# Layer 2's block stages: the bound of k plus u on VectorE in place of GpSimd, and new orders of both stages' work

## The chip, the cores and the metric

The kernel runs on one core of a Trainium2 chip: TensorE (PE), VectorE (DVE), ScalarE (ACT), GpSimd (POOL) and SyncE (SP), which issues most of the DMAs. The metric is the time of one execution on the device in microseconds; lower is better. Names as in the code: P = 128 partitions, TIME = 512 time steps, CH = 512 channels, BATCH = 4, UNITS = 16 units of a recurrence (4 groups of 128 channels by 4 batches), NB = 39 blocks of 128 token slots.

## What is computed

Four layers in a row change x of 4 x 512 x 512 float32. Each one runs a bidirectional decayed recurrence (WKV) over time, gates it with the sigmoid of x and puts the result through a feed-forward part that is added to x. Layer 2's feed-forward part is a mixture of 8 experts of which each token takes two. The recurrence reads the same k and v in every layer; v is k here.

```python
ek  = exp(minimum(k, 30)); ekv = ek * v
# nf, df: a = a*decay + ekv_t, b = b*decay + ek_t over time; nb, db: the same backwards
euk = exp(minimum(u + k, 30))
num = nf + nb - ekv + euk * v
den = df + db - ek + euk
out = sigmoid(r) * (num / maximum(den, 1e-8)) * (0.8 + 0.2 * tf)

# layer 2, feed-forward
scores = softmax(x @ W_gate.T); w, i = top_k(scores, 2)
eo = (silu(x @ gate_proj) * (x @ up_proj)) @ down_proj     # for each expert
y  = sum(eo[i] * w / sum(w)) + x
```

The backward scan is written so that it leaves out the step's own term, so no ekv and ek are subtracted.

## The kernel before

`experts` is layer 2's feed-forward part, from routing to the experts' outputs. It first routes the tokens and writes them to DRAM sorted by expert, in 39 blocks of 128 slots. Then come the two block stages that the change touches.

The gate/up stage, A, has eight turns (A_TURNS) of five blocks. A block is loaded from DRAM (`load_block`, into one of three buffers moe_zt), transposed on TensorE (`cols_of_z`), split into a high and a low part (`z_high` on ScalarE, `z_low` on VectorE), multiplied with the expert's gate and up weights in 12 matmuls (`gate_up`), gated (`silu` on ScalarE, `hidden` on VectorE) and written to DRAM (`store_hidden`, from one of two buffers moe_sg). A passage loads and splits the down weights, which lie in x's place meanwhile, since x is parked in DRAM; SyncE fetches them in eight pieces of 512 KB, one at the end of each of the turns 1 to 8 (`load_down`).

The down stage, B, has eight turns of five blocks too: `load_hidden` (four buffers moe_hb, 128 KB each), `cols_of_h` (two transposes), `h_high` and `h_low`, six matmuls (`down`), `out` on ScalarE (three buffers, those of moe_zt) and `store_out` (256 KB). At the end of the turns 1 to 4 SyncE issues `unpark`, which brings back a quarter of x, 1 MB.

Beside the blocks both stages carry layer 3's recurrence, one unit of 128 x 512 a turn: `w` eight units in A with one set of buffers, `v` eight units in B with two sets, which lie in columns of wh and wl, so that the trace calls its tiles moe_wh and moe_wl. A unit's steps, by engine: SyncE loads k (`load_k`, line 408) and exp_k and exp_k times v (`load_ek`, 414 and 415), 256 KB each; the bound `eu = min(k + u, 30)` (`bound`, 470); the exponential on ScalarE (`exps`, 349); GpSimd's product eu * k (`products`, 359), its sum into the forward numerator (`num_u`, 397) and with the backward one (`num_later`, 403); on VectorE the forward and backward scans (`scan_alone`, 384 and 389), the sum of both denominators (`both`, 476) and with eu (`den`, 482); ScalarE's `take_den`, `ln`, `recip_exp` (498, 506, 515); VectorE's `newton` (524, 526) and `quotient` (532); SyncE's `store` of the ratio (541), 256 KB.

The order on each engine is written out by hand. Each engine runs one loop over turns j, and `block_a(j, lag, q)` or `block_b(j, lag, q)` is block q of five of turn j - lag, or none; `unit_a` and `unit_b` are the same for units. So "third block" below is q = 2 of lag 1, and the next turn's first is q = 0 of lag 0. Every step waits for the semaphores of what it reads and of the buffer that it writes. All waits and issues of an engine are in order: on SyncE a DMA behind a waiting one waits too. The DMAs of SyncE share one queue (q1). `bound` waits for k and, of the unit that had the buffer before, for `den` and `newton`; `load_ek` waits for that unit's scans, `load_k` for its `num_u`, `load_block` for `cols_of_z` three blocks before, `load_hidden` for `cols_of_h` four before, `silu` for the hidden store two before, `h_high` and `h_low` for `down` two before.

## Time and profile before

| | us |
|---|---|
| timed runs | 1832.17, 1837.15, 1837.28 |
| their median | 1837.15 |
| the profiled execution | 1831.05 |
| its span, first to last instruction | 1829.2 |
| busy in the span: TensorE, VectorE, ScalarE, GpSimd | 1535.8, 1177.8, 983.6, 390.8 |
| mean granted clock of TensorE | 0.925 |

The span is one execution by the hardware profiler. Busy shares are means over four layers with different limits, so for a change in two stages the stages' own windows are read, and the waits in them.

### The profile page before, as it was taken

Reading aid. Unit: us, or ns where it says so; the run is one execution under the profiler, and the core shown is the slowest. Engines: PE = TensorE matmul, PEld = TensorE weight load, DVE = VectorE, ACT = ScalarE, POOL = GpSimd, SP = SyncE. Lnnn points to the kernel's source line nnn. Section 1 sums busy time; section 2 is a strip of 40 time slices with the busy share of each in tenths; the row PEclk is TensorE's granted clock in tenths of the full one; section 3 lists DMA queues with packets and bytes.
Section 4 is the critical chain, followed back from the end, with each engine's and each line's share of the span. In section 5 each row is a group of like instructions: output and inputs, shape, how many; then the busy total and the mean of one; then the engine's idle time right before and its main releaser. Section 6 shows DMA issues by size and latency. Waiting matters only on the chain. (4 is left out here: it accounts for less than half of the span.)

```text
span 1829.2 us, 21312 instructions
## 1 busy us (share of the span) xinstructions
PE 1535.8 (84%) x6839; PEld 1060.4 (58%) x6872; DVE 1177.8 (64%) x1888; ACT 983.6 (54%) x1313; POOL 390.8 (21%) x283
## 2 busy tenths in 40 slices
PE   5665778899977999996379957739999999999997
PEld 2222334444434666656357745538888888888886
DVE  7998688899987999986747777855422222222222
ACT  6764788899966999975246754524321221121210
POOL 0000111111200000004823334662032312322211
PEclk9998888899998999995579978979999999999999
DMA  7864633212103333327765648673010001101002
GB/s 282 278 197 166 241 104 104 81 59 69 53 12 128 120 104 109 113 75 267 281 198 188 201 158 277 240 253 115 1 35 35 35 1 35 35 0 35 1 12 81
DMA packets 117904, 218.54 MB, mean 119 GB/s; under 512 B 12708, under 2 KB 39588, under 8 KB 115364
## 3 DMA queue, kind: packets, MB, share of 16 engines
q1 hardware_dynamic: 112100, 199.34, 32.1%
q0 software_dynamic: 5120, 16.78, 2.6%
q8 instruction: 59, 0.97, 0.2%
q10 hardware_dynamic: 576, 1.05, 0.2%
q14 instruction: 49, 0.40, 0.1%
HBM read 149.10 MB, written 68.03 MB: 119 GB/s over the span
## 5 line engine op out<-in xcount | busy, mean ns | idle before, releaser
L2534 ACT ACTIVATE ffn_h<-ffn_pg,ffn_gate_chunk 128x512 f32<-128x512 f32 x64 | 44.0, 687 | 324.5 <-PE ffn_pg L2611 275.6
L2697 DVE SCALAR_TENSOR_TENSOR ffn_h<-ffn_pu,ffn_up_scale,ffn_h 128x512 f32<-128x512 f32 x64 | 48.1, 751 | 231.6 <-PE ffn_pu L2611 231.5
L2707 DVE SCALAR_TENSOR_TENSOR x<-ffn_po,ffn_out_scale,x 128x512 f32<-128x512 f32 x128 | 87.2, 744 | 149.3 <-PE ffn_po L2630 149.3
L2585 POOL TENSOR_TENSOR ffn_hl<-ffn_h,ffn_hh 128x512 fp32r<-128x512 f32 x64 | 82.5, 1289 | 413.2 <-ACT ffn_hh L2541 413.2
L960 POOL TENSOR_TENSOR l_rr<-l_rr,constants 128x1 f32<-128x1 f32 x32 | 28.8, 901 | 482.8 <-DVE l_rr L987 482.8
L2630 PE MATMUL ffn_po<-ffn_hh,ffn_wh 128*128 128x512 f32 x256 | 101.1, 395 | 3.5 <-DVE x L2707 2.9
L2611 PE MATMUL ffn_pg<-zhi,ffn_wh 128*128 128x512 f32 x256 | 101.6, 397 | 0.0
L2611 PE MATMUL ffn_pg<-zhi,ffn_wl 128*128 128x512 f32 x256 | 101.2, 395 | 0.0
L2611 PE MATMUL ffn_pu<-zhi,ffn_wh 128*128 128x512 f32 x256 | 101.1, 395 | 0.0
L2611 PE MATMUL ffn_pu<-zhi,ffn_wl 128*128 128x512 f32 x256 | 101.1, 395 | 0.0
L2611 PE MATMUL ffn_pu<-zlo,ffn_wh 128*128 128x512 f32 x256 | 101.1, 395 | 0.0
L2611 PE MATMUL ffn_pg<-zlo,ffn_wh 128*128 128x512 f32 x256 | 101.0, 395 | 0.0
L2630 PE MATMUL ffn_po<-ffn_hh,ffn_wl 128*128 128x512 f32 x256 | 100.6, 393 | 0.0
L2630 PE MATMUL ffn_po<-ffn_hl,ffn_wh 128*128 128x512 f32 x256 | 100.2, 392 | 0.0
L2195 POOL TENSOR_TENSOR x<-x,moe_zr 128x512 f32<-128x512 f32 x16 | 21.8, 1380 | 302.5 <-DVE moe_zr L2237 302.4
L2541 ACT ACTIVATE ffn_hh<-ffn_h 128x512 fp32r<-128x512 f32 x64 | 40.1, 627 | 83.5 <-DVE ffn_h L2697 83.5
L1965 PE MATMUL moe_bank<-moe_wh,moe_zhi 128*128 x156 | 65.1, 417 | 0.7 <-ACT moe_zhi L2093 0.7
L1965 PE MATMUL moe_bank<-moe_wh,moe_zlo 128*128 x156 | 62.5, 401 | 0.0
L1965 PE MATMUL moe_bank<-moe_wl,moe_zhi 128*128 x156 | 62.4, 400 | 0.0
L369 DVE TENSOR_TENSOR_SCAN wkv_fd<-decay,wkv_ek 128x512 f32<-128x512 f32 x48 | 58.4, 1216 | 2.9 <-DMA wkv_ekv<-exp_k_times_v 2.9
L814 PE MATMUL l_pa<-l_row_b,l_diag 128*128 128x512 f32 x128 | 58.2, 597 | 2.4 <-ACT l_diag L890 2.4
L369 DVE TENSOR_TENSOR_SCAN wkv_fn<-decay,wkv_ekv 128x512 f32<-128x512 f32 x48 | 58.4, 1216 | 0.0
(381 smaller groups left out, 4412.3 us busy)
## 6 DMA issues: line engine op xcount, KB each, us to landing
wkv_k<-in_fside SPq DMA_DIRECT2D x56, 256.0 KB, 3.7
ratio<-wkv_fn SPq DMA_DIRECT2D x56, 256.0 KB, 2.1
wkv_ek<-exp_k SPq DMA_DIRECT2D x40, 256.0 KB, 3.3
wkv_ekv<-exp_k_times_v SPq DMA_DIRECT2D x40, 256.0 KB, 3.9
moe_zt<-tokens_by_slot SPq DMA_DIRECT2D x39, 256.0 KB, 3.2
expert_out<-moe_zt SPq DMA_DIRECT2D x39, 256.0 KB, 2.3
moe_wl<-in_moe_up SPq DMA_DIRECT2D x16, 512.0 KB, 8.2
ffn_raw<-in_gated SPq DMA_DIRECT2D x8, 1024.0 KB
```

Of the source, the lines that this page charges most:

```text
L369: eng.tensor_tensor_scan(forward[:, :], decay.to_broadcast([P, TIME]), values[:, :], 0.0, op0=ALU.mult, op1=ALU.add)
L814: eng.matmul(p_a[:, m * 512:(m + 1) * 512], diag[p][:, :], rows["b1"][:, m * 512:(m + 1) * 512], start=True, stop=False)
L960: eng.tensor_tensor(out[p][:, :], out[p][:, :], c["minus_half"][:, :], ALU.pow).then_inc(*E(name).inc)
L1965: last = eng.matmul(p_gu[j % DEEP][:, :], z[j % 2][:, k * P:(k + 1) * P], part[:, k, ds(at, WCOL)], start=n == 0, stop=n == 3 * CT - 1)
L2195: eng.tensor_tensor(x_unit(n), x_unit(n), zr[n % ZRS][:, :], ALU.add).then_inc(*E("x_plus_z").inc)
L2534: eng.activation(hf[t][:, :], p_g[t][:, :], ACT.Silu, scale=scale).then_inc(*E(f"silu{t}").inc)
L2541: eng.activation(hh[t][slot % 2][:, :], hf[t][:, :], ACT.Copy).then_inc(*E(f"hh{t}").inc)
L2585: eng.tensor_tensor(hl[t][slot % 2][:, :], hf[t][:, :], hh[t][slot % 2][:, :].bitcast(F32), ALU.subtract).then_inc(*E(f"hl{t}").inc)
L2611: last = eng.matmul(ps[:, :], chunk_w(part, slot, which, k, t), z[:, k, tok], start=(n == 0), stop=(n == 3 * CT - 1))
L2630: last = eng.matmul(p_o[:, o, :], chunk_w(w, slot, "down", k, o), h[k][slot % 2][:, :], start=(n == 0), stop=(n == 3 * HT - 1))
L2697: eng.scalar_tensor_tensor(hf[t][:, :], p_u[t][:, :], scale, hf[t][:, :], ALU.mult, ALU.mult).then_inc(*E(f"h{t}").inc)
L2707: last = eng.scalar_tensor_tensor(x[:, o, :], p_o[:, o, :], out_s[:, o:o + 1], x[:, o, :], ALU.mult, ALU.add)
```

## The change

On VectorE `bound` is added in both stages and on GpSimd it is removed. In A it stands behind `quotient`, in B it is done one turn earlier than before (lag 0), between `both` and `den`. GpSimd runs `products`, `num_u` and `num_later` of a unit in that order in both stages. In B `exps` moves from near the front of ScalarE's turn to near its end, the last backward scan of a unit to the start of VectorE's next turn, and the ratio's store from the middle of SyncE's turn of lag 3 to the end of that of lag 2, ahead of `unpark`. The loads of k and exp_k, the stores of hidden and output blocks, and a few steps of TensorE and ScalarE change places as the diff shows. No computation changes.

```diff
--- before.py
+++ after.py
@@ -1845,24 +1845,24 @@
                     load_block(n)
                 for n in block_a(j, 1, 3):
                     load_block(n)
+                for n in block_a(j, 1, 4):
+                    load_block(n)
+                for u in unit_a(j, 1):
+                    w.load_k(eng, u, u % w.slots)
                 for u in unit_a(j, 1):
                     w.load_ek(eng, u, u % w.slots)
-                for n in block_a(j, 1, 4):
-                    load_block(n)
+                for n in block_a(j, 2, 4):
+                    store_hidden(n)
+                for n in block_a(j, 1, 0):
+                    store_hidden(n)
                 for n in block_a(j, 0, 0):
                     load_block(n)
-                for n in block_a(j, 2, 4):
-                    store_hidden(n)
-                for u in unit_a(j, 1):
-                    w.load_k(eng, u, u % w.slots)
-                for u in unit_a(j, 2):
-                    w.store(eng, u, u % w.slots)
-                for n in block_a(j, 1, 0):
-                    store_hidden(n)
                 for n in block_a(j, 0, 1):
                     load_block(n)
                 for n in block_a(j, 1, 1):
                     store_hidden(n)
+                for u in unit_a(j, 2):
+                    w.store(eng, u, u % w.slots)
                 for n in block_a(j, 1, 2):
                     store_hidden(n)
                 for n in block_a(j, 1, 3):
@@ -1870,33 +1870,33 @@
                 if 1 <= j <= DOWN_PIECES:
                     load_down(j - 1)
             eng.wait_ge(*E("gate_up").at(NB - 1))
-            for j in range(B_TURNS + 3):
+            for j in range(B_TURNS + 2):
                 for n in block_b(j, 1, 2):
                     load_hidden(n)
                 for n in block_b(j, 1, 3):
                     load_hidden(n)
+                for u in unit_b(j, 0):
+                    v.load_k(eng, u, u % v.slots)
                 for n in block_b(j, 1, 4):
-                    load_hidden(n)
-                for u in unit_b(j, 3):
-                    v.store(eng, u, u % v.slots)
-                for n in block_b(j, 0, 0):
-                    load_hidden(n)
-                for u in unit_b(j, 0):
-                    v.load_ek(eng, u, u % v.slots)
-                for n in block_b(j, 0, 1):
                     load_hidden(n)
                 for n in block_b(j, 2, 4):
                     store_out(n)
-                for u in unit_b(j, 0):
-                    v.load_k(eng, u, u % v.slots)
+                for n in block_b(j, 0, 0):
+                    load_hidden(n)
                 for n in block_b(j, 1, 0):
                     store_out(n)
                 for n in block_b(j, 1, 1):
                     store_out(n)
+                for n in block_b(j, 0, 1):
+                    load_hidden(n)
+                for u in unit_b(j, 0):
+                    v.load_ek(eng, u, u % v.slots)
                 for n in block_b(j, 1, 2):
                     store_out(n)
                 for n in block_b(j, 1, 3):
                     store_out(n)
+                for u in unit_b(j, 2):
+                    v.store(eng, u, u % v.slots)
                 if 1 <= j <= BATCH:
                     unpark(j - 1)
             v.stored(eng)
@@ -2024,10 +2024,10 @@
                     cols_of_z(n)
                 for n in block_a(j, 1, 1):
                     gate_up(n)
+                for n in block_a(j, 1, 2):
+                    gate_up(n)
                 for n in block_a(j, 1, 4):
                     cols_of_z(n)
-                for n in block_a(j, 1, 2):
-                    gate_up(n)
                 for n in block_a(j, 1, 3):
                     gate_up(n)
                 for n in block_a(j, 0, 0):
@@ -2049,10 +2049,10 @@
                     cols_of_h(n)
                 for n in block_b(j, 1, 2):
                     down(n)
+                for n in block_b(j, 0, 0):
+                    cols_of_h(n)
                 for n in block_b(j, 1, 3):
                     down(n)
-                for n in block_b(j, 0, 0):
-                    cols_of_h(n)
                 for n in block_b(j, 1, 4):
                     down(n)
 
@@ -2128,10 +2128,10 @@
                 if j == A_TURNS + 1:
                     for m in range(FIRST_DOWN):
                         down_high(m)
+                for n in block_a(j, 1, 1):
+                    z_high(n)
                 for u in unit_a(j, 2):
                     w.take_den(eng, u, u % w.slots)
-                for n in block_a(j, 1, 1):
-                    z_high(n)
                 for u in unit_a(j, 2):
                     w.ln(eng, u, u % w.slots)
                 for n in block_a(j, 1, 2):
@@ -2163,28 +2163,28 @@
                     h_high(n)
                 for u in unit_b(j, 2):
                     v.take_den(eng, u, u % v.slots)
-                for u in unit_b(j, 1):
-                    v.exps(eng, u, u % v.slots)
-                for n in block_b(j, 1, 2):
-                    h_high(n)
                 for u in unit_b(j, 2):
                     v.ln(eng, u, u % v.slots)
                 for n in block_b(j, 1, 0):
                     out(n)
+                for n in block_b(j, 1, 2):
+                    h_high(n)
                 for n in block_b(j, 1, 3):
                     h_high(n)
+                for n in block_b(j, 1, 1):
+                    out(n)
                 for u in unit_b(j, 2):
                     v.recip_exp(eng, u, u % v.slots)
-                for n in block_b(j, 1, 1):
+                for n in block_b(j, 1, 2):
                     out(n)
                 for n in block_b(j, 1, 4):
                     h_high(n)
-                for n in block_b(j, 1, 2):
-                    out(n)
+                for u in unit_b(j, 1):
+                    v.exps(eng, u, u % v.slots)
+                for n in block_b(j, 0, 0):
+                    h_high(n)
                 for n in block_b(j, 1, 3):
                     out(n)
-                for n in block_b(j, 0, 0):
-                    h_high(n)
                 for n in block_b(j, 1, 4):
                     out(n)
 
@@ -2212,21 +2212,17 @@
             first_set_over(eng)
             for j in range(A_TURNS + 1):
                 for u in unit_a(j, 1):
-                    w.bound(eng, u, u % w.slots)
-                for u in unit_a(j, 1):
                     w.products(eng, u, u % w.slots)
                 for u in unit_a(j, 1):
                     w.num_u(eng, u, u % w.slots)
                 for u in unit_a(j, 1):
                     w.num_later(eng, u, u % w.slots)
-            for j in range(B_TURNS + 2):
-                for u in unit_b(j, 1):
-                    v.bound(eng, u, u % v.slots)
-                for u in unit_b(j, 2):
+            for j in range(B_TURNS + 0):
+                for u in unit_b(j, 0):
+                    v.products(eng, u, u % v.slots)
+                for u in unit_b(j, 0):
                     v.num_u(eng, u, u % v.slots)
-                for u in unit_b(j, 1):
-                    v.products(eng, u, u % v.slots)
-                for u in unit_b(j, 2):
+                for u in unit_b(j, 0):
                     v.num_later(eng, u, u % v.slots)
 
         @block.vector
@@ -2379,40 +2375,44 @@
                     z_low(n)
                 for u in unit_a(j, 2):
                     w.newton(eng, u, u % w.slots)
+                for n in block_a(j, 1, 0):
+                    hidden(n)
                 for u in unit_a(j, 2):
                     w.quotient(eng, u, u % w.slots)
-                for n in block_a(j, 1, 0):
+                for u in unit_a(j, 1):
+                    w.bound(eng, u, u % w.slots)
+                for n in block_a(j, 1, 1):
                     hidden(n)
+                for n in block_a(j, 1, 3):
+                    z_low(n)
                 for u in unit_a(j, 1):
                     w.scan_alone(eng, u, u % w.slots, "scan_d", False)
-                for n in block_a(j, 1, 3):
-                    z_low(n)
-                for n in block_a(j, 1, 1):
-                    hidden(n)
                 for u in unit_a(j, 1):
                     w.scan_alone(eng, u, u % w.slots, "scan_d", True)
-                for u in unit_a(j, 1):
-                    w.both(eng, u, u % w.slots)
                 for n in block_a(j, 1, 4):
                     z_low(n)
                 for n in block_a(j, 1, 2):
                     hidden(n)
+                for u in unit_a(j, 1):
+                    w.both(eng, u, u % w.slots)
                 for n in block_a(j, 1, 3):
                     hidden(n)
-                for u in unit_a(j, 1):
-                    w.scan_alone(eng, u, u % w.slots, "scan_n", False)
                 for n in block_a(j, 0, 0):
                     z_low(n)
                 for u in unit_a(j, 1):
                     w.den(eng, u, u % w.slots)
                 for u in unit_a(j, 1):
-                    w.scan_alone(eng, u, u % w.slots, "scan_n", True)
+                    w.scan_alone(eng, u, u % w.slots, "scan_n", False)
                 for n in block_a(j, 1, 4):
                     hidden(n)
+                for u in unit_a(j, 1):
+                    w.scan_alone(eng, u, u % w.slots, "scan_n", True)
             for m in range(FIRST_DOWN, DOWN_PIECES):
                 down_low(m)
             v.set_ends(eng)
             for j in range(B_TURNS + 2):
+                for u in unit_b(j, 2):
+                    v.scan_alone(eng, u, u % v.slots, "scan_n", True)
                 for n in block_b(j, 1, 1):
                     h_low(n)
                 for u in unit_b(j, 1):
@@ -2424,21 +2424,21 @@
                 for n in block_b(j, 1, 3):
                     h_low(n)
                 for u in unit_b(j, 1):
-                    v.both(eng, u, u % v.slots)
-                for u in unit_b(j, 1):
-                    v.den(eng, u, u % v.slots)
-                for n in block_b(j, 1, 4):
-                    h_low(n)
-                for u in unit_b(j, 1):
                     v.scan_alone(eng, u, u % v.slots, "scan_n", False)
                 for u in unit_b(j, 2):
                     v.newton(eng, u, u % v.slots)
+                for n in block_b(j, 1, 4):
+                    h_low(n)
+                for u in unit_b(j, 2):
+                    v.quotient(eng, u, u % v.slots)
+                for u in unit_b(j, 1):
+                    v.both(eng, u, u % v.slots)
+                for u in unit_b(j, 0):
+                    v.bound(eng, u, u % v.slots)
+                for u in unit_b(j, 1):
+                    v.den(eng, u, u % v.slots)
                 for n in block_b(j, 0, 0):
                     h_low(n)
-                for u in unit_b(j, 1):
-                    v.scan_alone(eng, u, u % v.slots, "scan_n", True)
-                for u in unit_b(j, 2):
-                    v.quotient(eng, u, u % v.slots)
 
 
 def gated_ffn(core, c, d, ratio):
```

## Rows read from the trace of the kernel before

**Rows 1.** Chain of waits, 900 to 1210 us: start us, us, what.

```profile
1200.78 0.34 SPq L1543
```

**Rows 2.** Windows: stretch, length, busy (count) PE, PEld, DVE, ACT, POOL; PEclk, DMA, GB/s.

```profile
926.00:1068.00 142.00, 132.76 (x624) 105.53 (x624) 102.42 (x145) 93.03 (x138) 46.83 (x30) 0.97 0.60 187
...
1087.00:1198.50 111.50, 79.85 (x308) 56.64 (x308) 88.21 (x115) 52.52 (x108) 60.27 (x32) 0.87 0.69 236
```

**Rows 3.** The same view by turn in stage A.

```profile
950.00:968.70 18.70, 17.27 (x87) 13.76 (x85) 13.57 (x19) 13.06 (x20) 6.30 (x5) 1.00 0.64 201
...
1042.00:1060.00 18.00, 17.86 (x88) 14.45 (x87) 14.81 (x22) 13.26 (x20) 6.11 (x4) 1.00 0.68 215
```

**Rows 4.** Waits in stage A: waiter, releaser, us in total, times, longest.

```profile
PE moe_bank L1951 <- DMA moe_zt<-tokens_by_slot: 30.4, 10, 23.7
```

**Rows 5.** Timeline, TensorE in A: start, us, engine, line, operation [idle before <- releaser].

```profile
992.53 0.66 PE L1951 MATMUL moe_bank<-ident,moe_zt 128*128 128x128 f32 x4 [1.85 <-DMA moe_zt<-tokens_by_slot]
```

**Rows 6.** Timeline, SyncE's issues in the next turn of A.

```profile
1004.08 0.33 SPq L414 DMA_DIRECT2D wkv_ek<-exp_k  x1
...
1005.63 1.45 SPq L1808 DMA_DIRECT2D moe_zt<-tokens_by_slot  x2
...
1007.12 0.43 SPq L1812 DMA_DIRECT2D expert_hidden<-moe_sg  x1
```

**Rows 7.** Windows view by turn in stage B.

```profile
1098.90:1113.40 14.50, 10.35 (x39) 7.73 (x38) 8.86 (x14) 6.31 (x14) 4.28 (x3) 0.76 0.77 254
...
1142.00:1158.00 16.00, 12.03 (x43) 8.77 (x42) 10.61 (x16) 6.72 (x14) 7.62 (x5) 0.79 0.78 266
...
1170.00:1182.00 12.00, 9.83 (x41) 6.33 (x41) 11.66 (x15) 6.73 (x14) 8.40 (x5) 1.00 0.71 242
```

**Rows 8.** Timeline, TensorE in B, the third of four waits.

```profile
1132.28 0.69 PE L1980 MATMUL moe_bank<-ident,moe_hb 128*128 128x128 f32 x2 [2.85 <-DMA moe_hb<-expert_hidden]
```

**Rows 9.** Timeline, SyncE in the same turn of B.

```profile
1126.11 0.53 SPq L1794 DMA_DIRECT2D x<-x_park  x1
...
1126.75 1.76 SPq L1818 DMA_DIRECT2D moe_hb<-expert_hidden  x3
...
1129.50 0.32 SPq L541 DMA_DIRECT2D ratio<-moe_wl  x1
```

**Rows 10.** DMA landing of line 1794 (x returns), then of line 1822 (output blocks).

```profile
DMA to landing us min/median/max: 5.7/6.0/6.6
...
DMA to landing us min/median/max: 2.0/2.3/4.2
```

**Rows 11.** Line views: count, duration ns min/median/max, first and last start.

```profile
L341 DVE TENSOR_SCALAR wkv_eu<-wkv_k,u x48: 473/478/486, 10.5 to 791.2; 128x512 f32<-128x512 f32 x48
...
L470 POOL TENSOR_SCALAR moe_wh<-moe_wh,u x8: 2127/2980/2982, 1086.7 to 1180.8; 128x512 f32<-128x512 f32 x8
...
L476 DVE TENSOR_TENSOR moe_wl<-moe_wl x8: 681/684/1405, 1093.5 to 1186.8; 128x512 f32<-128x512 f32 x8
...
L482 DVE TENSOR_TENSOR moe_wl<-moe_wl,moe_wh x8: 691/692/1653, 1094.2 to 1188.3; 128x512 f32<-128x512 f32 x8
...
L532 DVE SCALAR_TENSOR_TENSOR moe_wl<-moe_wl,neg_gain x8: 720/1034/1035, 1113.8 to 1197.5; 128x512 f32<-128x512 f32 x8
```

**Rows 12.** ScalarE's waits in B.

```profile
ACT moe_wh L349 <- POOL moe_wh L470: 14.5, 7, 2.6
```

**Rows 13.** Timeline in a waiting turn of B, ScalarE and TensorE.

```profile
1123.78 0.39 ACT L2105 ACTIVATE moe_hhi<-moe_bank 128x256 fp32r<-128x256 f32 x1 [0.28 <-PE moe_bank L1996]
...
1124.06 0.59 ACT L2111 ACTIVATE moe_zt<-moe_bank 128x512 f32<-128x512 f32 x1
...
1124.92 0.38 PE L1980 MATMUL moe_bank<-ident,moe_hb 128*128 128x128 f32 x2
```

**Rows 14.** Timeline, VectorE at the end of B.

```profile
1186.53 0.39 DVE L2338 TENSOR_TENSOR moe_hlo<-moe_bank,moe_hhi 128x256 fp32r<-128x256 f32 x1
...
1197.52 0.75 DVE L532 SCALAR_TENSOR_TENSOR moe_wl<-moe_wl,neg_gain 128x512 f32<-128x512 f32 x1
```

## Prediction

> **What bounds the kernel now.** I read the page's chain first: it is followed back from the end and holds no line of layer 2. The block of layer 2 ends for all engines together; SyncE then issues the next layer's first load at 1200.78 us [rows 1], and everything behind it follows from there. So a microsecond won before that is a microsecond won at the end. Then the windows view by stages: the gate/up stage (A) runs from 926 to 1068 us, a passage follows in which the down weights are split, and the down stage (B) from 1087 to 1198.5 us [rows 2]. The diff touches A and B.
>
> **Stage A.** TensorE is the busy engine, 132.8 of 142 us [rows 2]. One block is 12 matmuls and 4 transposes, 16 instructions. Four windows from 950 to 1024 us, about a turn of five blocks each, hold 87, 82, 82 and 83 of them: 20.9 blocks in 74 us, 3.54 us each; the two after them, to 1060 us, hold 88 each: 11 blocks in 36 us, 3.27 us each (the rows show the first and the last of the six) [rows 3]. The difference is waiting. TensorE waits 30.4 us for token blocks, 23.7 of it for the stage's first, so 6.7 us inside it [rows 4]. The longest is 1.85 us at a turn's fifth block [rows 5]. The SyncE timeline tells why one is late: in the next turn the load of the fifth block stands behind the two loads of exp_k, which go out at 1004.08, when the last scan is through; so it is issued at 1005.63 with 512 KB ahead of it, and the late hidden block is stored at 1007.12 only [rows 6].
>
> **Stage B.** Two regimes. In the four turns from 1098.9 to 1158 us a turn takes 13.6 to 16 us and VectorE is busy for 8.9 to 10.6 of it; in the two from 1158 to 1182 VectorE is busy 11.7 of 12.0 us (the rows show the first and the last of the four, and the second of the two) [rows 7]. The first kind waits for a DMA: TensorE stands 3.58, 3.62, 2.85 and 3.29 us at the turn's third block (the third is shown) [rows 8]. Its load is issued at 1126.75, straight behind the 1 MB that brings x back (1126.11), and TensorE goes on at 1132.28 [rows 8, 9], 5.5 us after the issue where 256 KB can land in 2.0 [rows 10]. The four waits match the four transfers of x, which land in 5.7 to 6.6 us [rows 10]. With them gone the stage is VectorE's.
>
> **The change part by part.**
>
> *Bound on VectorE.* Elsewhere VectorE does the same 128x512 instruction in 0.478 us; GpSimd takes 2.98 for it in B [rows 11]. In A VectorE is busy 13.6 of 18.7 us [rows 3], so the 0.48 hide: zero. In B they hide in the four waiting turns and count in the three after them, and once ahead of the first low part, for which the first down product waits: 4 x 0.48 = **+1.9 us**. The upper bound: it could wait for a running GpSimd instruction as others do. The sum on line 482 takes 0.69 us alone and up to 1.65, so 0.48 + 0.96 = 1.44 us each [rows 11].
> What goes away: ScalarE waited 14.5 us for the bound in seven turns of B [rows 12]. In the waiting turns that lies inside TensorE's wait for the DMA, in the late ones VectorE had work all the time: zero.
> What VectorE pays to GpSimd: in a late turn line 476 takes 0.72 us more than alone, line 482 0.96, the quotient (line 532) 0.31 [rows 11], 2.0 in all. After the change GpSimd's products and numerator sum follow the exponential, which now stands late in ScalarE's turn, just where VectorE does quotient, both, bound and den. So the 2.0 stay. At best the two sums' 1.68 go, 5.0 us in three turns.
> The Trainium skill's page "SBUF — State Buffer", section "SBUF: two separate sides", says that VectorE and GpSimd take a shared port pair exclusively, so that the one that starts second blocks until the other is through. The 1.4 us of line 476, twice its 0.68 alone, agree with that. By that rule the moved bound could be blocked in its turn; with 1.44 us each the sum below would be 3.8 us larger.
>
> *Order in A.* The fifth block's load goes ahead of the recurrence's loads, the loads of k ahead of exp_k's, the store of the late hidden block ahead of two loads, the fifth block's transposes one product later on TensorE. The last scan goes behind the last hidden product, 0.4 us, and exp_k's loads wait that much longer, with nobody at them for 5 us. The ratio's write-back now passes in front of two hidden stores; the ratio is ready by then. If the 20.9 slow blocks run at 3.35 us, (3.54 - 3.35) x 20.9 = 4.0 us come back; at 3.27, 5.6; at least nothing, since the third block's load still follows the last hidden store and a weight load. I take **-4.0**.
>
> *Passage.* The same instructions behind the same last weight load: zero.
>
> *Order in B, the four turns in which x returns.* The chain is: the third block's transposes, the products, `out` of the turn's fourth block, its store, x's return, the load, its landing. Three things come into it. (a) ScalarE now does h_high of the next turn's first block ahead of that `out`, 0.28 us from its start to the next one's, and TensorE its transposes ahead of the fourth product, 0.38: 0.66 us [rows 13]. (b) SyncE issues the ratio's write-back between store and return, 0.32 us and a gap of 0.1 [rows 9]; before, it stood behind the three loads. (c) Its 256 KB drain ahead of the load. From 2.3 us for 256 KB and 6.0 for 1 MB [rows 10] it is 3.7 x 256/768 = 1.23 us; at the 254 and 266 GB/s of the rows' waiting turns [rows 7], it is 1.0, and less if the transfers overlap. I take 0.85; bounds 0 and 1.23. The first return has only (a), as no ratio is done by then, the other three have all: 0.66 + 3 x (0.66 + 0.42 + 0.85) = **+6.4**.
>
> *Tail.* From the last low part (1186.53) VectorE works 11.74 us until 1198.27 [rows 14]. Now come low part 0.34, scan 1.13, Newton 1.37, quotient 0.75 to 1.03, both 1.40 and den 1.65 if GpSimd meets them, then ScalarE's three steps, 2.2 with their gaps, Newton 1.37 and quotient 0.75: 10.6 to 11.2. I take **-0.6**.
>
> Sum: 1.9 - 4.0 + 6.4 - 0.6 = **+3.7 us**.
>
> **Against which time.** The profiled execution took 1831.05 us, 1.85 more than its span of 1829.2; the timed runs took 1832.17, 1837.15 and 1837.28. The profile lies 6.1 under their median. I set the sum against the middle of all four, 1834.7: **1838.4 us**. A measurement of this kernel can tell about 0.3%, 5.5 us, from no change.
>
> **Rivals.**
> *The write-back also delays the late turns (slower).* Place: the third block's load in the turns without x's return. It now has 0.66 + 0.42 + 0.85 = 1.9 us in front of it. From the point at which that makes it land later than VectorE's turn of 12.0 us needs it, TensorE stops there, at up to 1.9 us in three turns, 5.7; I take 4.5: 1842.9. For it: the DMA engines are 0.71 busy there [rows 7], and the load of k, which waits for GpSimd's numerator sum, is new ahead of the fourth block's. Against: TensorE has no such wait there now.
> *GpSimd lets VectorE be and the write-back costs nothing (faster).* The two sums run alone, -5.0; of B's chain only 4 x 0.66 = 2.6 stay; A returns 5.6; bound and tail as above: -5.6 + 2.6 - 5.0 + 1.9 - 0.6 = -6.7, 1828.0. For it: GpSimd's work in B falls by 2.98 us a turn. Against: its two sums follow the exponential closely.
> *It does nothing:* A's waits move to another block and B's keep their length, 1834.7. For it: the waits in A at a turn's third block hang on the last hidden store, which isn't issued earlier.
>
> **How the numbers follow.** Forecast 0.34, nothing 0.08, slower rival 0.30, faster rival 0.28; so within 0.3% 0.42, slower 0.30, faster 0.28. The forecast's own range is 1833.7 to 1840.2 (-1 to +5.5). As cases of both signs hold most of the chance, the whole range goes from just under the faster rival, 1827, to A at zero with B's full sum and most of the slower rival: 1834.7 + 7.7 + 4.5 = 1847.
>
> **What would show it.** A: in SyncE's timeline the fifth block's load right behind the fourth's; no wait of 1.85 us; the stage 138 us instead of 142. B: still four waits of TensorE for moe_hb, nearer 5 than 3.3 us, in turns of 15 to 16; line 470 on VectorE at 0.48; late turns of 12.5 us full of VectorE. Wrong if the four waits shrink (then the queue was not the chain), if lines 476 and 482 stay at 0.69 late in B (the faster rival), or if waits for moe_hb appear after 1160 us (the slower one).

## The result and the profile after

The changed kernel takes **1846.95 us** (median of six runs, 1844.12 to 1849.94), the kernel before 1836.85 (six runs, 1832.17 to 1841.37). The ratio is 1.0062, interval 1.0043 to 1.0081: **10.1 us slower**, where I had forecast 1838.4 with a range of 1827 to 1847 and 0.30 for slower. The forecast was 3.7 us on a base of 1834.7, which itself lay 2.2 us under the median of six.

The two traces lie further apart than the medians. The profiled execution of after took 1849.94 us with a span of 1848.1, 3.0 over its median; that of before lies 5.8 under the median of its now six runs. 10.1 + 3.0 + 5.8 = 18.9 us, which is the difference of the spans. The stages account for it so (A from the start of the first transposes to that of the last gate/up product, B from the start of the first down product to that of the last, the tail from there to SyncE's first issue for the next layer; all are read from starts given to 0.1 us):

| us | A and passage | B | tail | all the rest |
|---|---|---|---|---|
| before | 161.4 | 100.8 | 12.4 | 1554.6 |
| after | 159.7 | 117.9 | 12.1 | 1558.4 |

The rest holds nothing that the change touches, and moves between 1554.6 and 1567.1 us in the sixteen traces of this study. So experiments below are compared by their stages first, with the timed runs beside them. Two traces of the same code, `a_new_b_old` and `a_new_again`, have B and tail at 114.3 and 114.9 us.

Windows view of after: gate/up stage, passage, down stage, then four turns of the down stage, two in which x returns and the two late ones (columns as in rows 2):

```profile
928.00:1068.70 140.70, 132.90 (x624) 105.36 (x624) 106.80 (x153) 94.66 (x138) 34.47 (x22) 0.97 0.61 190
1068.70:1087.50 18.80, 1.38 (x4) 0.58 (x4) 14.46 (x21) 11.71 (x14) 3.35 (x2) 0.60 0.42 136
1087.50:1215.50 128.00, 86.53 (x308) 60.75 (x308) 101.25 (x118) 53.90 (x108) 34.56 (x24) 0.81 0.63 204
...
1101.90:1119.60 17.70, 10.72 (x41) 7.29 (x41) 12.70 (x17) 6.95 (x14) 4.21 (x4) 0.90 0.73 230
1119.60:1138.40 18.80, 12.00 (x40) 8.58 (x40) 13.09 (x17) 6.95 (x14) 4.50 (x4) 0.69 0.70 225
...
1172.80:1185.90 13.10, 10.31 (x42) 7.16 (x40) 12.56 (x16) 6.85 (x14) 4.12 (x4) 0.89 0.69 222
1185.90:1199.40 13.50, 10.53 (x41) 7.34 (x41) 12.61 (x16) 6.85 (x14) 4.11 (x4) 0.88 0.68 221
```

The turns with x's return took 13.6 to 16 us before, by the prediction's reading of [rows 7], and 16.8 to 18.8 now; the late ones grew from 12.0 to 13.1 and 13.5. The DMA share of the stage fell from 0.69 to 0.63 [rows 2]: the same bytes, over a longer time.

TensorE still waits four times for a hidden block, as in [rows 8]; timeline of after, the second of the four:

```profile
1124.65 0.69 PE L1980 MATMUL moe_bank<-ident,moe_hb 128*128 128x128 f32 x2 [4.25 <-DMA moe_hb<-expert_hidden]
```

and its load in SyncE's timeline (to set against [rows 9]):

```profile
1112.02 0.39 SPq L414 DMA_DIRECT2D moe_wh<-exp_k  x1
1112.46 0.42 SPq L415 DMA_DIRECT2D moe_wh<-exp_k_times_v  x1
1112.94 1.79 SPq L1822 DMA_DIRECT2D expert_out<-moe_zt  x2
1115.22 0.32 SPq L541 DMA_DIRECT2D ratio<-moe_wl  x1
1115.58 0.54 SPq L1794 DMA_DIRECT2D x<-x_park  x1
1116.21 1.62 SPq L1818 DMA_DIRECT2D moe_hb<-expert_hidden  x2
```

In this turn 9.1 us lie between the issue of x's return (1115.58) and TensorE's going on (1124.65), where the turn of [rows 8, 9] had 1132.28 - 1126.11 = 6.2. What stands ahead of the return was issued in the last 3.6 us: 512 KB of exp_k and its product, two output blocks, 256 KB of the ratio. x itself lands later than the 5.7 to 6.6 us of [rows 10], by the view of line 1794 of after:

```profile
DMA to landing us min/median/max: 7.6/8.2/8.6
```

These two points, the issue of line 1794 and TensorE's start behind the wait, cut the four turns into parts. I read them off the same two timelines for every return:

| us | first product to first return | return to TensorE, four times | TensorE to the next return, three times |
|---|---|---|---|
| before | 9.2 | 6.2, 7.0, 6.2, 6.6 | 8.5, 7.7, 7.6 |
| after | 10.4 | 8.6, 9.1, 8.7, 8.1 | 8.9, 9.7, 8.9 |
| difference | +1.2 | +8.5 | +3.7 |

Together +13.4 us (1087.61 to 1146.45 before, 1087.77 to 1159.98 after). From there to the last product come 3.8 more.

The four waits themselves hardly grew: 4.14, 4.25, 2.92 and 2.33 us make 13.6, where it was 13.3 before. The load lands later, but TensorE also gets to it later. In each of these turns it now stops for a low part on the way, 1.66 to 2.15 us, where in before it had no such stop above 0.7. VectorE and TensorE in the turn shown above:

```profile
1117.79 0.41 DVE L2334 TENSOR_TENSOR moe_hlo<-moe_bank,moe_hhi 128x256 fp32r<-128x256 f32 x1
...
1118.40 0.49 PE L1996 MATMUL moe_bank<-moe_wh,moe_hhi 128*128 x1 [1.66 <-ACT moe_hhi L2105]
```

This stop costs nothing here, as it lies inside the time from the return to the landing of the load. It also means that the length of these waits doesn't tell how late the load is.

### The profile page after: what moved, and what is told of

It is laid out like the page before. It is cut to its first block and busy times, and to the rows that moved or that the text cites. A ratio compares the mean times of both kernels' runs of the same rounds, so it can differ in the third digit from the quotient of the medians.

```text
span 1848.1 us, 21309 instructions
## 1 busy us (share of the span) xinstructions
PE 1547.2 (84%) x6839; PEld 1065.9 (58%) x6872; DVE 1195.7 (65%) x1904; ACT 986.9 (53%) x1313; POOL 354.2 (19%) x267
## 5 line engine op out<-in xcount | busy, mean ns | idle before, releaser
L1996 PE MATMUL moe_bank<-moe_wh,moe_hhi 128*128 x78 | 42.1, 539 | 20.0 <-issue 14.6
```

The source lines that it names most:

```text
L1996: last = eng.matmul(p_eo[j % DEEP][:, :], h[j % 2][:, k * P:(k + 1) * P], part[:, k, ds(at, CH)], start=n == 0, stop=n == 3 * HT - 1)
```

## The experiments

All ratios are against the kernel before, timed between them on the same chip.

**The stages apart.** Stage A of after, stage B of before, on all five engines (diffs are against after, where nothing else is said):

```diff
 # stage A: as in the change; stage B, SyncE (the other engines alike):
-            for j in range(B_TURNS + 2):
+            for j in range(B_TURNS + 3):
...
-                for u in unit_b(j, 2):
-                    v.store(eng, u, u % v.slots)
```

> Stage A of the changed kernel, stage B of the kernel before. Both theories put the loss in stage B: 1 to 3 us faster than before (stage A is 1.8 us shorter in the trace of the change, from its first block to the first down product). If stage A carries part of the loss, it comes out slower than before.

It took 1831.65 us, ratio 0.9955 (0.9938 to 0.9971), by its medians 5.5 us faster where 1 to 3 were expected. I ran the same code again beside later kernels:

> New stage A, old stage B, once more and in more rounds, beside the one with halves. My prediction gave stage A 4.0 us, bounds 0 and 5.6. The first measure gave a ratio of 0.9955 from four runs; the traces give 157.8 us on the mean of eight kernels against 161.4 in the one of before. Expected: 2 to 5 us faster than before, 0.997 to 0.999.

1829.88 us, 0.9978 (0.9965 to 0.9990). So stage A's order gains 4 to 8 us by the two timings, and B's loses more than the whole difference. In the traces A and passage take 161.4 us before and 156.1 to 159.7, mean 157.5, in the fifteen with the new A: 3.9 less. After's own waits in A:

```profile
PE moe_bank L1951 <- DMA moe_zt<-tokens_by_slot: 28.0, 6, 23.5
```

4.5 us inside the stage where [rows 4] had 6.7. After's own 159.7 is the longest of the fifteen, 1.7 less than before; the mean is the better estimate of what the order gives.

**SyncE's order in B undone.** After, with SyncE's loop for B as before (exp_k's loads ahead of all of the turn's output stores, the write-back behind the three loads; the cut shows these two moves, the others follow the kernel before) and all other engines new:

```diff
-            for j in range(B_TURNS + 2):
+            for j in range(B_TURNS + 3):
...
+                for u in unit_b(j, 3):
+                    v.store(eng, u, u % v.slots)
                 for n in block_b(j, 0, 0):
                     load_hidden(n)
+                for u in unit_b(j, 0):
+                    v.load_ek(eng, u, u % v.slots)
...
-                for u in unit_b(j, 2):
-                    v.store(eng, u, u % v.slots)
                 if 1 <= j <= BATCH:
                     unpark(j - 1)
```

> The changed kernel, with only SyncE's order in stage B as it was before; the other engines keep the new one. Queue theory (the loads of exp_k behind the second output store, and the ratio's write-back ahead of x's return, pile up in the DMA queue and x's return lands in 8.2 instead of 6.0 us): 6 to 10 us of the 10 come back, the four turns with x's return are 14 to 15 us again. Engine theory (VectorE's both, bound and den meet GpSimd's sums ahead of the low part that the next product waits for): 0 to 3 us come back.

1836.99 us, 0.9992 (0.9977 to 1.0008). B and tail take 118.6 us instead of 130.0. The return takes 6.4, 6.7, 6.5 and 7.1 us to TensorE, as before, and the four waits shrink to 1.66, 0.96, 0.38 and 0.84, since the stop for the low part stays. From the first product to the fourth wait's end it takes 60.1 us (before 58.8, after 72.2), from there to the last product 46.5 (before 41.9, after 45.8): SyncE's order is what costs in the four turns, and the other engines' order what costs in the late ones.

**Its two moves, one at a time.** First exp_k's loads alone put back, ahead of the store of the turn's own first block:

```diff
                 for n in block_b(j, 0, 0):
                     load_hidden(n)
+                for u in unit_b(j, 0):
+                    v.load_ek(eng, u, u % v.slots)
                 for n in block_b(j, 1, 0):
                     store_out(n)
                 for n in block_b(j, 1, 1):
                     store_out(n)
                 for n in block_b(j, 0, 1):
                     load_hidden(n)
-                for u in unit_b(j, 0):
-                    v.load_ek(eng, u, u % v.slots)
```

> The changed kernel with one move: SyncE issues the loads of exp_k of stage B ahead of the first output store instead of behind the next turn's second hidden load. Queue theory: x's return lands in 6 to 7 us instead of 8.2, each of the four turns is 1.5 to 2.5 us shorter, 5 to 9 us in all. Engine theory: within 1 us of the changed kernel.

1840.68 us, 1.0015 (1.0003 to 1.0027); B and tail 121.4. Its timeline of SyncE:

```profile
1103.09 0.42 SPq L414 DMA_DIRECT2D moe_wh<-exp_k  x1
1103.57 0.56 SPq L415 DMA_DIRECT2D moe_wh<-exp_k_times_v  x1
1104.37 6.36 SPq L1822 DMA_DIRECT2D expert_out<-moe_zt  x2
...
1111.90 2.27 SPq L1822 DMA_DIRECT2D expert_out<-moe_zt  x2
1114.60 0.95 SPq L541 DMA_DIRECT2D ratio<-moe_wl  x1
1115.59 0.53 SPq L1794 DMA_DIRECT2D x<-x_park  x1
```

and TensorE's wait for that turn:

```profile
1122.17 0.44 PE L1980 MATMUL moe_bank<-ident,moe_hb 128*128 128x128 f32 x2 [2.44 <-DMA moe_hb<-expert_hidden]
```

This is the clearest row of the study. The ratio's write-back is still right ahead of x's return, but the return now takes 1122.17 - 1115.59 = 6.6 us to TensorE, and 6.9, 6.8 and 6.7 in the other three turns: mean 6.7 against 8.6 of after and 6.5 of before. exp_k's 512 KB, issued 12 us ahead of the return, fill a stretch in which SyncE waits 6.36 us for output blocks; in after they go out 3.6 us ahead and are still on the way.

Then the write-back alone put back:

```diff
-            for j in range(B_TURNS + 2):
+            for j in range(B_TURNS + 3):
...
                 for n in block_b(j, 1, 4):
                     load_hidden(n)
+                for u in unit_b(j, 3):
+                    v.store(eng, u, u % v.slots)
...
-                for u in unit_b(j, 2):
-                    v.store(eng, u, u % v.slots)
```

> The changed kernel with one move: SyncE's write-back of the ratio in stage B stands behind the three hidden loads of the next turn, as before, instead of ahead of x's return. My prediction priced it at 0.42 + 0.85 us in three turns: 3.8 us faster than the changed kernel. If the exp_k loads are the larger part of the pile-up: 1 to 3 us. Engine theory: within 1 us.

1847.22 us (1840.61 to 1850.88, four runs), 1.0048 (1.0031 to 1.0065). In its trace B and tail take 122.6 us, 7.4 less than after; but that execution took 1840.61 us, the shortest of the four, and the other three 1846.3 to 1850.9. By the ratios it is 2.6 us faster than after. So the trace may overstate this move, and four runs don't settle it. The return takes 8.8, 6.3, 7.9 and 8.3 us to TensorE. The first of them has no write-back in either kernel and is as long as after's 8.6: exp_k's loads alone give the long value. The other three take 7.5 in the mean against after's 8.6: beside late exp_k loads the write-back is worth about 1.1 us in this trace, against the 0.2 beside early ones.

Both put back, which leaves the other orders of SyncE new:

```diff
...
+                for u in unit_b(j, 3):
+                    v.store(eng, u, u % v.slots)
...
+                for u in unit_b(j, 0):
+                    v.load_ek(eng, u, u % v.slots)
                 for n in block_b(j, 1, 0):
                     store_out(n)
...
```

> The changed kernel with both moves of SyncE undone in stage B: exp_k's loads ahead of the output stores and the write-back behind the hidden loads. Stage B and its tail last 130.0 us in the trace of the changed kernel, 121.4 with the first move undone, 122.6 with the second, 118.6 with SyncE's whole old order. If the two pile up in one queue they overlap in what they cost: 118 to 120 us. If they add: 114.

1836.67 us, 1.0002 (0.9988 to 1.0015), B and tail 117.9: all that SyncE wholly old gives. Alone the two gave 8.6 and 7.4 in the traces, together 12.1, an overlap of 3.9. By the timed ratios they give 8.6 and 2.6, together 11.0, and simply add. As the 7.4 comes from that one short execution, the overlap isn't shown.

**The other half: SyncE new, the rest of B old** (VectorE, ScalarE, TensorE and GpSimd as before, the bound on GpSimd):

```diff
 # stage A and SyncE's stage B as in the change; GpSimd in stage B:
+                for u in unit_b(j, 1):
+                    v.bound(eng, u, u % v.slots)
 # VectorE in stage B:
-                for u in unit_b(j, 0):
-                    v.bound(eng, u, u % v.slots)
```

> Fourth corner of a square in stage B (stage A new in all four): SyncE in the new order, the other engines in the old one, the bound on GpSimd. The other corners: both old 1831.7, SyncE old with new engines 1837.0, both new 1847. Queue theory, the two parts simply add: SyncE's order costs 10 us here too, 1840 to 1843. If the loss needs both (the new order of SyncE only hurts because ScalarE's outputs come in another order): 1832 to 1836.

1852.64 us, 1.0086 (1.0052 to 1.0120), where 1840 to 1843 or 1832 to 1836 were expected: neither theory saw it. B and tail are 133.7 us: the slowest of all. TensorE waits 5.48, 7.11, 6.82 and 7.45 us, and in late turns too; timeline of TensorE:

```profile
1177.52 0.44 PE L1980 MATMUL moe_bank<-ident,moe_hb 128*128 128x128 f32 x2 [2.61 <-DMA moe_hb<-expert_hidden]
```

The record shows what is added here. SyncE's waits in B, and its timeline ahead of the second return:

```profile
SPq L541 <- DVE moe_wl L532: 20.6, 6, 3.4
...
1112.50 0.40 SPq L414 DMA_DIRECT2D moe_wh<-exp_k  x1
...
1113.43 0.99 SPq L1822 DMA_DIRECT2D expert_out<-moe_zt  x2
1117.87 0.32 SPq L541 DMA_DIRECT2D ratio<-moe_wl  x1
1118.23 0.53 SPq L1794 DMA_DIRECT2D x<-x_park  x1
```

The old order of VectorE has the quotient (line 532) as its turn's last step. SyncE stands at the write-back until the quotient is there, 20.6 us in six turns, and x's return and the hidden loads stand behind it; in after the same wait sums to 1.3 us. From TensorE's start to the next return it takes 36.1 us in three turns where after has 27.4. The return itself is not long: 8.1 us the first time, with exp_k's loads issued 2.3 us ahead of it, then 6.8, 6.4 and 7.0, with the loads 5.7 to 6.3 us ahead and the write-back right ahead. So the loads are cheap again once they are some 6 us old, and a write-back alone in front costs next to nothing in queue time.

With B and tail 114.3 (all old), 118.6 (engines new), 133.7 (SyncE new) and 130.0 (both), the orders depend on each other: in the traces the engines' new order costs 4.3 us beside the old SyncE and wins 3.7 beside the new. The timed ratios have the same signs, but the win isn't clear of noise: 1.0086 (1.0052 to 1.0120) and 1.0062 (1.0043 to 1.0081) overlap.

**The bound by itself.** In the old orders of B, the bound on VectorE right behind its Newton step (diff against `a_new_again`):

```diff
 # GpSimd
-                for u in unit_b(j, 1):
-                    v.bound(eng, u, u % v.slots)
 # VectorE
                     v.newton(eng, u, u % v.slots)
+                for u in unit_b(j, 0):
+                    v.bound(eng, u, u % v.slots)
```

> New stage A, stage B with every order as before, and in it only the bound moved: on VectorE behind Newton's steps, one turn earlier, instead of on GpSimd. My prediction: 0.48 us a turn where VectorE is full, up to 1.44 if it meets GpSimd, and the quotient 0.3 shorter: 0 to 2 us slower than the same kernel without the move (1831.7), so 1831 to 1834. Rival, the bound's release of ScalarE (14.5 us of waits in seven turns) was on the path after all: 1827 to 1830.

1836.47 us, 1.0000 (0.9983 to 1.0017); B and tail 114.0, no longer than the 114.3 and 114.9 without it. Inside B it does cost: from the fourth wait to the last product it takes 44.6 us against 40.7 and 41.9, and the tail gives it back, 10.3 against 12.4. The timed ratio lies above `a_new_again`'s 0.9978, whose interval it meets, and above the first timing's 0.9955, whose interval it doesn't. The best estimate is a cost of some 4 us where 0 to 2 were expected. In the new orders, with SyncE as in `sp_old` (diff against it), the bound back on GpSimd:

```diff
 # GpSimd
                 for u in unit_b(j, 0):
+                    v.bound(eng, u, u % v.slots)
+                for u in unit_b(j, 0):
                     v.products(eng, u, u % v.slots)
 # VectorE
-                for u in unit_b(j, 0):
-                    v.bound(eng, u, u % v.slots)
```

> SyncE's old order, the new orders of the other engines in stage B, but the bound back on GpSimd at the start of its turn. Against the same kernel with the bound on VectorE (1837.0). If the engine part of the loss (5 us) is the bound on VectorE, in its place between both and den: 1832 to 1834. If it is the order of the low parts and sums: 1836 to 1838.

1835.87 us, 1.0007 (0.9992 to 1.0023), against 1836.99 for `sp_old`: not told apart by time. In the trace 115.6 against 118.6; from the fourth wait to the last product 44.2 against 46.5.

**The low part that had got behind.** In after's late turns TensorE stops about 2 us for the low part of the next turn's first block (shown under the late turns, below). I moved it ahead, in `sp_old`:

```diff
                     v.quotient(eng, u, u % v.slots)
+                for n in block_b(j, 0, 0):
+                    h_low(n)
                 for u in unit_b(j, 1):
                     v.both(eng, u, u % v.slots)
...
-                for n in block_b(j, 0, 0):
-                    h_low(n)
```

> SyncE's old order, new orders of the other engines in stage B, with one move: VectorE does the low part of the next turn's first block ahead of both, bound and den instead of behind them. In the trace TensorE waits 1.7 to 2.7 us in every turn for that low part. If this is the engine part of the loss: 3 to 6 us faster than 1837.0. If VectorE's own sum of work sets the turn, the order inside the turn gives nothing: 1836 to 1838.

1840.53 us (1834.30 to 1848.29), 1.0038 (1.0017 to 1.0058); B and tail 120.7 against 118.6. A miss: 3 to 6 us less were expected, and by the ratios it is some 8 us slower than `sp_old` (1.0038 against 0.9992, intervals apart). The waits for hidden blocks came back at 4.23, 4.32, 3.71 and 5.90 us: taking the one wait away moved the turn's time into the next one. In the trace 2 us came on top, and its fourth return took 8.3 us with exp_k's loads 11 us old.

**x's return out of the way.** With the old B (diff against `a_new_again`), x in halves (512 KB in each of eight turns), behind the load of k and ahead of the first output store of the turn:

```diff
-            def unpark(b):
-                if b == 0:
+            def unpark_half(n):
+                b, k = n // 2, n % 2 * 2
+                if n == 0:
...
                     v.load_k(eng, u, u % v.slots)
+                if 1 <= j <= 2 * BATCH:
+                    unpark_half(j - 1)
                 for n in block_b(j, 1, 0):
                     store_out(n)
...
-                if 1 <= j <= BATCH:
-                    unpark(j - 1)
```

> New stage A, old stage B, and x's return in eight halves of 512 KB, one in each turn 1 to 8, issued behind the load of k instead of at the turn's end ahead of the hidden loads. If the four waits for moe_hb (3.5 us each in the traces) are made by the return that stands ahead of the load, they vanish and the turns go down to VectorE's 12 us: 6 to 12 us faster than the same kernel with whole returns (about 1832). If the queue's total of bytes sets the turns, wherever they stand: within 2 us of it.

1832.16 us, 0.9983 (0.9969 to 0.9997), not told apart from `a_new_again`, where 6 to 12 us less were expected. The waits for hidden blocks are gone, yet B and tail take 117.2 us: another wait took their place, ScalarE's for the output stores, which now queue behind x:

```profile
ACT moe_zt L2112 <- DMA expert_out<-moe_zt: 24.3, 11, 4.3
```

The same halves in after's own orders, behind the load of the turn's first hidden block:

```diff
                 for n in block_b(j, 0, 0):
                     load_hidden(n)
+                if 1 <= j <= 2 * BATCH:
+                    unpark_half(j - 1)
...
-                if 1 <= j <= BATCH:
-                    unpark(j - 1)
```

> The changed kernel with x's return in eight halves of 512 KB, issued ahead of the first output store of the turns 1 to 8. If SyncE's new order costs only because its bytes stand ahead of the 1 MB and the hidden loads behind it, most of the 11 us between the two orders go, 1836 to 1840. If the new order also starves the queue in mid-turn whatever returns, 1842 to 1846.

1831.59 us, 0.9977 (0.9963 to 0.9992), better than the 1836 to 1840 expected: **15 us under after with the bytes, the engines' orders and the bound unchanged.** B and tail take 111.2 us instead of 130.0, one short wait for a hidden block is left, and VectorE is full where x returns; windows view of two turns:

```profile
1136.00:1148.00 12.00, 8.74 (x38) 5.20 (x36) 11.97 (x16) 5.97 (x12) 3.66 (x4) 1.00 0.86 272
1148.00:1160.00 12.00, 9.74 (x42) 6.51 (x43) 11.96 (x15) 6.85 (x14) 3.52 (x4) 1.00 0.92 299
```

Is it the size of a half or the place? The whole 1 MB at that same place:

```diff
                 for n in block_b(j, 0, 0):
                     load_hidden(n)
+                if 1 <= j <= BATCH:
+                    unpark(j - 1)
                 for n in block_b(j, 1, 0):
                     store_out(n)
...
-                if 1 <= j <= BATCH:
-                    unpark(j - 1)
```

> The changed kernel with one move: x's return, whole (1 MB, turns 1 to 4), behind the five hidden loads and ahead of the first output store, where the halves stood. Halving and moving together took 15 us off. If it is the place (the bytes that SyncE's new order gathers, and then the return, stand ahead of the third block's load): stage B and tail near 111 to 115 us, 1831 to 1835. If it is the size of the piece: 1840 to 1847.

1833.35 us, 0.9984 (0.9966 to 1.0002), B and tail 111.4: **the place**. Its timeline of SyncE:

```profile
1110.05 0.38 SPq L1818 DMA_DIRECT2D moe_hb<-expert_hidden  x1
1110.48 0.53 SPq L1794 DMA_DIRECT2D x<-x_park  x1
1112.68 3.85 SPq L1822 DMA_DIRECT2D expert_out<-moe_zt  x2
1116.94 0.32 SPq L1818 DMA_DIRECT2D moe_hb<-expert_hidden  x1
```

and the landing of line 1794:

```profile
DMA to landing us min/median/max: 7.0/8.1/9.1
```

x lands as late as in after, 8.1 us against 8.2, but the next load of a hidden block is 6.5 us behind it in this turn, where in after two follow at once.

**Both findings together.** `after_halves` (diff against it) with the bound of B on GpSimd, as in `bound_pool_new`:

```diff
 # GpSimd
                 for u in unit_b(j, 0):
+                    v.bound(eng, u, u % v.slots)
+                for u in unit_b(j, 0):
                     v.products(eng, u, u % v.slots)
```

> The changed kernel with returns in halves, and the bound of stage B back on GpSimd at the start of its turn. VectorE is busy 11.1 to 12.0 of 12 us in the kernel with halves and the bound on VectorE. If VectorE now sets the turns, the bound's 0.48 to 1.5 us come back in eight turns: 3 to 8 us faster than 1831.6. If the bound hides, within 1.5 us. Prediction's price for it: 0.48 in the turns that VectorE fills.

**1826.63 us** (1821.08 to 1832.36, ten runs), 0.9945 (0.9928 to 0.9961), faster than both kernels; B and tail 107.2 us, 4.0 less than with the bound on VectorE. The ratios of the two, from different chips, differ by 0.0032, some 5.9 us, with intervals that just miss each other.

## Why the prediction failed, step by step

**What bounds the kernel: held.** The four waits hang on x's return, as read from [rows 8 to 10]: with the return moved, B and tail fall below those of before, 111 against 113.

**Stage A, -4.0: held in the mean.** A and passage together are 3.9 less in the mean of the traces, and 4 us less in the better of the two timings, 8 in the other; all traces are set against a single one of before. The fifth block's load goes out right behind the fourth's, ahead of k and exp_k, and the late hidden block is stored right behind exp_k's loads; in [rows 6] the block's load stood there, and the store behind it. SyncE in after:

```profile
1001.16 2.53 SPq L1808 DMA_DIRECT2D moe_zt<-tokens_by_slot  x3
1003.74 0.43 SPq L408 DMA_DIRECT2D wkv_k<-in_fside  x1
1004.37 0.33 SPq L414 DMA_DIRECT2D wkv_ek<-exp_k  x1
...
1005.22 4.30 SPq L1812 DMA_DIRECT2D expert_hidden<-moe_sg  x2
```

The sign "138 us instead of 142" did not come: in one and the same measure the stage took 140.0 us before and 138.9 in after's own trace, 136.8 in the mean of the fifteen. So 3.2 of the 3.9 lie in the stage. **The passage, 0:** 21.5 before, 20.2 to 21.0 in all other traces, which is the rest.

**The four turns, +6.4: +13.4.** Terms (a) and (b), the issues and transposes between one wait and the next return, were 0.66 + 0.42 = 1.08 a turn; the table above has 3.7/3 = 1.2. In size they held; that it is these two isn't shown, for `sp_old` keeps the transposes and high part of term (a) and has 23.7 us in these three stretches, as before. The error is in what lies ahead of the load in the queue. **The step that failed is the one that isn't there:** in A the prediction followed exp_k's loads to their new place, but in B it named only the write-back, and gave no price to exp_k's two loads, 512 KB, which the diff moves from ahead of all of the turn's output stores to right ahead of its last two, so from some 10 us to some 4 us ahead of x's return. From return to TensorE after has 8.6 us in the mean, before 6.5, `ek_early` 6.7: of the 2.1 us, 1.9 go with exp_k's loads, in each of four turns, 7.6 us. By the method of term (c), 512 KB at the 254 GB/s of [rows 7] are 2.1 us: the sum needed only the row. In the other direction **(c) was too large** for a queue that is otherwise as before: the write-back's 256 KB were priced at 0.85, and 6.7 - 6.5 = 0.2 were measured beside early exp_k loads. Beside late ones, taking it away gave 1.1 in the trace of `store_behind`, so how the 2.1 us are shared out depends on which move comes first. With the missing row the prediction's own sum for the four turns would have been 6.4 + 4 x 2.1 = 14.8, where 13.4 were measured.

Of the signs named, two failed beside this: the four waits stayed at 13.6 us in all instead of growing to nearly 5 each, for the reason given under the table, and the turns took 16.8 to 18.8 us instead of 15 to 16.

That a fresh transfer ahead delays the load, and an old one doesn't, fits what the Trainium skill's page "DMA: Bandwidth & Descriptors", section "Queues, rings and completion order", says: on each DMA engine the descriptors of one issuing engine's queue are taken in the order of the ring. The traces agree: 8.6 us against 6.7 with nothing but exp_k's loads moved. They don't tell whether the load waits its turn or shares the bandwidth with what is still under way, and `hlow_first` has one return of 8.3 us without any such fresh loads.

**The late turns, +1.4 for three bounds: +3.8.** The prediction's 0.48 is what the bound takes when GpSimd leaves it alone. Line views of after, VectorE:

```profile
L470 DVE TENSOR_SCALAR wkv_eu<-wkv_k,u x8: 479/481/483, 939.3 to 1062.3; 128x512 f32<-128x512 f32 x8
L470 DVE TENSOR_SCALAR moe_wh<-moe_wh,u x8: 474/984/1519, 1086.7 to 1196.7; 128x512 f32<-128x512 f32 x8
...
L476 DVE TENSOR_TENSOR moe_wl<-moe_wl x8: 683/1764/1769, 1096.4 to 1208.3; 128x512 f32<-128x512 f32 x8
...
L482 DVE TENSOR_TENSOR moe_wl<-moe_wl,moe_wh x8: 678/679/1749, 1098.5 to 1210.0; 128x512 f32<-128x512 f32 x8
...
L384 DVE TENSOR_TENSOR_SCAN moe_wl<-decay,moe_wh x16: 1212/1218/2204, 1087.8 to 1204.1; 128x512 f32<-128x512 f32 x16
```

In A it is 0.48 each time, in B four times 0.47 or 0.48 and four times 1.49 to 1.52, 7.9 us in eight against 3.8; in the three late turns 1.49, 0.47 and 0.47. The upper bound of 1.44 was a real case. Of the late turns' loss the bound is about 2.3 us (46.5 against 44.2 in `sp_old` and `bound_pool_new`, beside the old SyncE); the rest belongs to the engines' orders. GpSimd and VectorE around the bound of the first late turn:

```profile
1168.72 1.53 POOL L397 TENSOR_TENSOR moe_wl<-moe_wl,moe_wh 128x512 f32<-128x512 f32 x1
1169.05 1.49 DVE L470 TENSOR_SCALAR moe_wh<-moe_wh,u 128x512 f32<-128x512 f32 x1
...
1172.68 1.27 POOL L403 TENSOR_TENSOR moe_wl<-moe_wl 128x512 f32<-128x512 f32 x1 [2.43 <-DVE moe_wl L389]
```

The Trainium skill's page "SBUF — State Buffer", section "SBUF: two separate sides", has a rule that fits: the two engines share a port pair, and where a VectorE instruction of the two-port mode or with two SBUF inputs needs it, the one that starts first holds it for its whole instruction. The traces agree: this bound starts inside GpSimd's sum of 1168.72 to 1170.25 and ends 0.3 us behind it, while the one at 1183.14 starts when GpSimd has been idle for 0.5 us and takes 0.47.

I said that VectorE's 2.0 us of blocked time would stay. They moved and grew, and they were 2.3 to begin with: the late turns of before also had a backward scan (line 389) of 1.55 us against 1.21 alone, which the prediction left out. Timeline of VectorE in a late turn:

```profile
1172.84 2.19 DVE L384 TENSOR_TENSOR_SCAN moe_wl<-decay,moe_wh 128x512 f32<-128x512 f32 x1
...
1180.09 1.43 DVE L532 SCALAR_TENSOR_TENSOR moe_wl<-moe_wl,neg_gain 128x512 f32<-128x512 f32 x1
1181.45 1.77 DVE L476 TENSOR_TENSOR moe_wl<-moe_wl 128x512 f32<-128x512 f32 x1
1183.14 0.47 DVE L470 TENSOR_SCALAR moe_wh<-moe_wh,u 128x512 f32<-128x512 f32 x1
1183.54 0.68 DVE L482 TENSOR_TENSOR moe_wl<-moe_wl,moe_wh 128x512 f32<-128x512 f32 x1
1184.14 0.41 DVE L2334 TENSOR_TENSOR moe_hlo<-moe_bank,moe_hhi 128x256 fp32r<-128x256 f32 x1
```

Line 482 is free (0.68, 0.96 less than in [rows 11]); line 476 takes 1.08 more than alone, the quotient 0.68, and a scan 0.97: 2.7 us against 2.3. That scan starts at 1172.84, just behind GpSimd's instruction at 1172.68 above. With the bound's 0.47 this makes the 0.9 by which VectorE's 12.56 busy us of 13.1 exceed the 11.66 of [rows 7]. So the **faster rival** saw half of it: one of its two sums did get free, and others paid. The last row above is the low part that TensorE waits for:

```profile
1184.75 0.66 PE L1996 MATMUL moe_bank<-moe_wh,moe_hhi 128*128 x1 [1.97 <-issue]
```

The profile names no releaser; that it is this low part follows from its end at 1184.55. The prediction didn't see it move behind both, bound and den, but `hlow_first` shows that moving it alone, there beside the old SyncE, wins nothing.

**The slower rival** (the write-back delays the late turns too) came near in size, 1842.9, by another way. That 1846.95 still lies under the range's top of 1847 is luck: the top was made of stage A at zero and of this rival's 4.5 us, and neither happened. Its sign was waits for hidden blocks after 1160 us; after's last one ends at 1159.98, that of the fourth return. Such late waits appear in `sp_new_eng_old` (2.61 us at 1177.52), where the write-back holds SyncE, and once in `hlow_first` (1.50 us).

**The tail, -0.6: -0.3.** The prediction's terms for it, with both sums blocked, add to 11.0 to 11.2; its lower end of 10.6 follows from none of them. The sum with the measured terms is -3.9 + 13.4 + 3.8 - 0.3 = 13.0 us, 3 more than the timed 10.1; it takes the mean of the traces for A, where after's own has 1.7, and one trace each for B and tail. This difference stays unexplained.

**What stays open.** The write-back's own share: 7.4 us of B in the trace of `store_behind`, 0 to 2.6 timed. What the engines' new orders cost in the late turns beside the bound's 2.3 us. And why `hlow_first` loses: 2 us in its trace, some 8 by the ratios. TensorE's granted clock fell with the longer stops, from 0.87 to 0.81 in the stage and from 1.00 to 0.88 in the late turns; no run tells what part of the 1.2 us between a wait and the next return, or of the late turns, comes from that.

## What to carry to other kernels

For each large transfer ahead of a load that an engine waits for, list what the same queue was given in the last few microseconds, both before and after the change, and price every DMA that crosses the line, the ones that the change only mentions in passing first: here two loads that nobody waited for cost more than the instruction the change is about. A big transfer that isn't urgent belongs right behind the urgent loads, ahead of a stretch in which the issuing engine must wait anyway; its own late landing costs nothing, as long as what is queued behind it can wait too. In `halves` it couldn't: ScalarE waited 24.3 us for output stores. And before a store is put ahead of urgent work on an engine that issues in order, look at when its data are ready: in `sp_new_eng_old` that alone held SyncE for 20.6 us. An instruction moved from GpSimd to VectorE has to be priced at what it costs beside GpSimd's remaining work, in the order that the change makes, not at what it costs alone.

## What the runs showed of the hardware that I had not expected

A scan of VectorE took up to 1 us more beside GpSimd: line 384 2.20 us against 1.21 alone, in seven of after's sixteen; in the kernel before line 384 was at most 1.36, but line 389 reached 2.21, as this view of before has it:

```profile
L389 DVE TENSOR_TENSOR_SCAN moe_wl<-moe_wh,decay x16: 1208/1214/2206, 1091.8 to 1193.2; 128x511 f32<-128x511 f32 x16
```

In the rows above an instruction is long when GpSimd is at work at its start; how busy GpSimd is in the whole stage, 34.6 us in after against 60.3, doesn't tell it. And the time of a 1 MB return to the 128 KB load behind it depended on the age of what was ahead of it: 6.5 to 6.7 us in the mean with exp_k's 512 KB 9 to 12.5 us old, 6.4 to 7.0 with them 5.7 to 6.3 us old, and 8.6 in the mean with them 2.8 to 3.9 us old.
